# A ring of eight weight tiles in the first expert layer, and the second expert layer's weights loaded during the attention

## The reference, cut to what matters

```
# layer 0, experts: 8 experts, 128 -> 512 -> 128
h = relu(einsum('tc,efc->tef', x, w1) + b1)
y = einsum('tef,ecf->tec', h, w2) + b2          # two of 8 taken by the router, weighted
# layer 1, attention: 128 -> 128
A, x_el, sidegate, gate = four projections of the RMS-normalized rows
h = gated_scan(A, x_el * sidegate); y = (gate * h) @ w_o + residual
# layer 1, experts: 16 experts, 128 -> 256 -> 128
mag, freq = fx @ bank_mag, fx @ bank_freq
hidden = tanh(mag) * cos(softplus(freq) + 0.1 + bank_phase)
out = hidden @ bank_down                         # two of 16, weighted, then RMS norm
```

## Time and profile before

| | |
|---|---|
| median of 3 runs | 742.98 us (738.69 to 751.54) |
| the profiled execution | 746.29 us |
| its span, first to last instruction | 744.5 us |
| mean granted TensorE clock | 0.855 |
| experts of layer 0, first to last tile | 312 to 447 us of the span |
| attention of layer 1 | 450 to 510 us |
| router and sorting for layer 1 | 510 to 556 us |
| experts of layer 1 | 556 to 722 us |

### The profile page before, as it was taken

The page is one execution under the profiler, slowest core; times in us unless marked ns, Lnnn a source line. Parts: engine busy times, 40 slices in busy tenths (PEclk is TensorE's granted clock), DMA queues, the critical chain, the costliest instruction groups (busy, mean ns, idle before and its releaser), DMA issues.

```text
span 744.5 us, 9210 instructions
## 1 busy us (share of the span) xinstructions
PE 547.2 (73%) x2152; PEld 331.9 (45%) x2153; DVE 489.2 (66%) x911; ACT 332.0 (45%) x643; POOL 437.8 (59%) x329
## 2 busy tenths in 40 slices
PE   8678899989988897747666794697476777478730
PEld 4223234334333334446656791255144565356620
DVE  4898988998997996613522245368832777755527
ACT  4637646745753641112122245745014867960004
POOL 0275999988989982165455545217046773067760
PEclk9979989989989997669899797989758999686785
DMA  5431534333333400246455644001001123311115
GB/s 175 131 99 61 169 115 165 101 107 115 102 113 99 127 15 25 71 115 174 156 162 167 193 150 120 0 1 29 28 25 47 37 41 21 113 43 42 43 48 164
DMA packets 45437, 69.05 MB, mean 93 GB/s; under 512 B 6162, under 2 KB 25460, under 8 KB 45268
## 3 DMA queue, kind: packets, MB, share of 16 engines
q1 hardware_dynamic: 39828, 57.17, 24.9%
q0 software_dynamic: 5568, 11.41, 6.1%
HBM read 59.45 MB, written 9.11 MB: 92 GB/s over the span
## 4 chain that ended last, share of the span: by engine, by line
PE 41%; DVE 22%; issue 11%; ACT 9%; another core or an unknown queue 9%; DMA 2%; POOL 2%; DVEq 2%; ACTq 1%; SPq 0%; POOLq 0%
PE ps L1084 9%; DVE hs L1691 7%; PE ps L1210 4%; PE ps L1392 3%; PE ps L1221 3%; PE ps L1047 3%; PE ps L1078 3%; PE ps L1261 2%; PE ps L1356 2%; DVE prod L1701 2%; PE ps L1381 2%; ACT ps L677 2%; PE ps L1000 1%; PE ps L1361 1%
## 5 line engine op out<-in xcount | busy, mean ns | idle before, releaser
L490 POOL TENSOR_TENSOR bu<-uT,b_sb 128x1024 f32<-128x1024 f32 x62 | 146.0, 2375 | 29.6 <-DMA b_sb<-b_rows 29.6
L462 POOL DMA_INDIRECT y_dram<-ys,rows_i x87 | 90.7, 1042 | 97.0 <-DVE ys L1787 43.8
L456 POOL DMA_INDIRECT xl<-h_dram,rows_i x87 | 91.6, 1053 | 69.1 <-DVE rows_i L1573 37.5
L1084 PE MATMUL ps<-prod,cst 128*128 128x512 f32 x256 | 129.9, 652 | 2.9 <-DVE yT L1711 2.9
L677 ACT ACTIVATE ps<-dtT,neg_a 128x512 f32<-128x512 f32 x128 | 85.6, 685 | 61.2 <-DVE hs L1691 60.4
L501 POOL TENSOR_TENSOR prod<-hs,c_sb 128x1024 f32<-128x1024 f32 x32 | 76.8, 2399 | 28.7 <-PE ps L1084 19.0
L1084 PEld LDWEIGHTS ps<-prod,cst 128*128 128x128 f32 x256 | 50.3, 207 | 81.7 <-issue 76.7
L1691 DVE TENSOR_TENSOR_SCAN hs<-ps,carry,bu 128x512 f32<-128x512 f32 x64 | 77.6, 1264 | 4.7 <-ACT ps L677 4.6
L1221 PE MATMUL ps<-w_s,ht 128*128 x312 | 49.5, 309 | 38.4 <-ACT ht L779 19.8
L1691 DVE TENSOR_TENSOR_SCAN hs<-ps,bu 128x512 f32<-128x512 f32 x64 | 73.9, 1206 | 4.8 <-ACT ps L677 4.7
L779 ACT ACTIVATE ht<-ps,b1T 128x128 f32<-128x128 f32 x78 | 24.3, 363 | 97.0 <-remote 49.2
(11 more groups left out here) (264 smaller groups left out, 956.7 us busy)
## 6 DMA issues: line engine op xcount, KB each, us to landing
b_sb<-b_rows SPq DMA_DIRECT2D x31, 512.0 KB, 4.5
w1r<-in_w SPq DMA_DIRECT2D x39, 256.0 KB
c_sb<-b_rows SPq DMA_DIRECT2D x32, 256.0 KB, 3.6
mf_s<-in_mf SPq DMA_DIRECT2D x16, 256.0 KB
w_s<-in_w SPq DMA_DIRECT2D x9, 256.0 KB, 4.0
h_dram<-h_tok SPq DMA_DIRECT2D x8, 256.0 KB
phase_s<-in_phase SPq DMA_DIRECT2D x16, 128.0 KB
down_s<-in_down SPq DMA_DIRECT2D x1, 2048.0 KB, 7.2
```

What stands on the lines that cost most here:

```text
L456: pool.indirect_dma_start(xl[:, j % slots, :], None, h_dram[l], bass.IndirectOffsetOnAxis(ap=rows_i[:, 0, j:j + 1], axis=0)).then_inc(load ...
L462: pool.indirect_dma_start(y_dram[l], bass.IndirectOffsetOnAxis(ap=rows_i[:, 1, j:j + 1], axis=0), ys[:, j % XR, :], None).then_inc(saved[j ...
L490: nc.gpsimd.tensor_tensor(bu[:, g % RING, :, :], uT[:, c % 2, :, :], b_sb[:, k % BRING, g % 2, :].unsqueeze(1).broadcast_to([P, ND, CHUNK] ...
L1084: last = nc.tensor.matmul(bank(Y_BANK + d), ident, prod[:, g % RING, d, :], start=n == 0, stop=n == NS - 1)
```

## The change

`WR` goes from 3 to 8: SP loads the weights of up to eight tiles ahead. The ring then takes all of the region up to `w2_s`; `wmod_s` and what follows it are placed on top of it, and `signs`, used during the stage, has a second copy `signs2` at the place of the (then unused) sorting tables. The semaphores of the b and c rows of the scan are used again for the ring. The 32 loads behind tiles 3 to 34 go; in their place SP issues 16 loads (8 of `mf_s` with 512 KB, 8 of `phase_s` with 256 KB) right behind the eight loads of `y0a` and `y0b`. ACT's two scalings move from the end of the expert stage to behind the last `columns_router`, ahead of the wait for `pick_exp`.

```diff
-WR = 3
+WR = 8
...
         w1r, e = place("w1r", [P, WR, F0], at=f0_at)
-        wmod_s, e = place("wmod_s", [P, 2, 6 * C], at=e)
+        assert e <= f0_at + E0 * F0 * 4
+        wmod_s, e = place("wmod_s", [P, 2, 6 * C], at=f0_at)
...
+        signs2, _ = place("signs2", [P, 2, BATCH, C], at=y0_at)
...
-        b_loaded = [sem(f"b_loaded{u}") for u in range(BRING)]
-        c_loaded = [sem(f"c_loaded{u}") for u in range(CRING)]
+        streamed = [sem(f"streamed{u}") for u in range(max(WR, BRING + CRING))]
...
-                sp.dma_start(w1r[:, j % WR, :], w1[:, bass.ds(e, 1), :].rearrange("p a f -> p (a f)")).then_inc(w1_loaded[j % WR], 16)
-                if WR <= j < WR + 2 * E1:
-                    es = slice((j - WR) // 2, (j - WR) // 2 + 1)
-                    if (j - WR) % 2 == 0:
-                        sp.dma_start(mf_s[:, es, :], mf[:, es, :]).then_inc(S["in_f1"], 16)
-                    else:
-                        sp.dma_start(phase_s[:, es, :], phase[es, :].partition_broadcast(P)).then_inc(S["in_phase"], 16)
+                sp.dma_start(w1r[:, j % WR, :], w1[:, bass.ds(e, 1), :].rearrange("p a f -> p (a f)")).then_inc(streamed[j % WR], 16)
...
             for c in range(NCHUNK):
                 load_rows(0, ST0, c, y0)
+            for e in range(0, E1, 2):
+                es = slice(e, e + 2)
+                sp.dma_start(mf_s[:, es, :], mf[:, es, :]).then_inc(S["in_f1"], 16)
+                sp.dma_start(phase_s[:, es, :], phase[es, :].partition_broadcast(P)).then_inc(S["in_phase"], 16)
...
-            act.wait_ge(S["in_f1"], 16 * E1)
-            act.wait_ge(S["in_phase"], 16 * E1)
-            nc.scalar.activation(mf_s[:, :, H1:2 * H1], mf_s[:, :, H1:2 * H1], ACT.Copy, scale=1.0 / (2 * PI)).then_inc(S["phase_done"], 1)
-            nc.scalar.activation(phase_s[:, :, :], phase_s[:, :, :], ACT.Identity, bias=eps_s[:, 2:3], scale=1.0 / (2 * PI)).then_inc(S["phase_done"], 1)
             act.preload_act_table_set(LOG_EXP)
...
             columns_router(3)
+            act.wait_ge(S["in_f1"], 16 * (E1 // 2))
+            act.wait_ge(S["in_phase"], 16 * (E1 // 2))
+            nc.scalar.activation(mf_s[:, :, H1:2 * H1], mf_s[:, :, H1:2 * H1], ACT.Copy, scale=1.0 / (2 * PI)).then_inc(S["phase_done"], 1)
+            nc.scalar.activation(phase_s[:, :, :], phase_s[:, :, :], ACT.Identity, bias=eps_s[:, 2:3], scale=1.0 / (2 * PI)).then_inc(S["phase_done"], 1)
             act.wait_ge(S["pick_exp"], 2)
```

More of the change, by code:

```diff
@@ L317, in adaln_two_layers, with rows_streamed, w1_streamed @@
         gathered = [sem(f"gathered{c}") for c in range(NCHUNK)]
-        b_loaded = [sem(f"b_loaded{u}") for u in range(BRING)]
-        c_loaded = [sem(f"c_loaded{u}") for u in range(CRING)]
+        streamed = [sem(f"streamed{u}") for u in range(max(WR, BRING + CRING))]
         saved = [sem(f"rows_out{u}") for u in range(XR)]
-        w1_loaded = [sem(f"w1_loaded{u}") for u in range(WR)]
+        def rows_streamed(u):
+            if u < BRING:
+                return len(range(u or BRING, PAIRS, BRING))
+            return len(range(u - BRING, PAIRS, CRING)) if u < BRING + CRING else 0
+        def w1_streamed(j):
+            return 16 * (rows_streamed(j % WR) + j // WR + 1)
         def rounds(l, u):
@@ L387, in _ @@
                     if k:
-                        sp.dma_start(b_sb[:, k % BRING, :, :], b_rows[c, n:n + 2, :].partition_broadcast(P)).then_inc(b_loaded[k % BRING], 16)
+                        sp.dma_start(b_sb[:, k % BRING, :, :], b_rows[c, n:n + 2, :].partition_broadcast(P)).then_inc(streamed[k % BRING], 16)
                     if k >= CRING:
                         sp.wait_ge(S["prod_pool"], k - CRING + 1)
-                    sp.dma_start(c_sb[:, k % CRING, :], b_rows[c, NS + n + 1, :].partition_broadcast(P)).then_inc(c_loaded[k % CRING], 16)
+                    sp.dma_start(c_sb[:, k % CRING, :], b_rows[c, NS + n + 1, :].partition_broadcast(P)).then_inc(streamed[BRING + k % CRING], 16)
                     for dst, src, done in later[k - 4:k - 3] if k >= 4 else ():
@@ L486, in inputs @@
                 k = g // 2
-                pool.wait_ge(b_loaded[k % BRING], 16 * (k // BRING + (1 if k % BRING else 0)))
+                pool.wait_ge(streamed[k % BRING], 16 * (k // BRING + (1 if k % BRING else 0)))
                 if g >= RING:
@@ L496, in products @@
                 k = g // 2
-                pool.wait_ge(c_loaded[k % CRING], 16 * (k // CRING + 1))
+                pool.wait_ge(streamed[BRING + k % CRING], 16 * (k // CRING + 1))
                 pool.wait_ge(S["scan_done"], 2 * g + 2)
@@ L1203, in up0 @@
                 pe.wait_ge(S["xt_sb0"], j + 1)
-                pe.wait_ge(w1_loaded[j % WR], 16 * (j // WR + 1))
+                pe.wait_ge(streamed[j % WR], w1_streamed(j))
                 if j >= 2:
@@ L1624, in one_more, with bounded @@
                 then(nc.vector.tensor_scalar(mod[:, l, :, k, :], mod[:, l, :, k, :], 1.0, None, ALU.add))
-            def bounded(l, k):
-                g, s0, s1 = mod[:, l, :, k, :], signs[:, 0, :, :], signs[:, 1, :, :]
+            def bounded(l, k, s):
+                g, s0, s1 = mod[:, l, :, k, :], s[:, 0, :, :], s[:, 1, :, :]
                 nc.vector.tensor_scalar(s0, g, 0.0, 2.0, ALU.is_ge, ALU.mult)
@@ L1737, in _ @@
                     one_more(0, CB)
-                    bounded(0, GA)
+                    bounded(0, GA, signs)
                 if g == 4:
@@ L1793, in attention_weights @@
                 one_more(1, CB)
-                bounded(1, GA)
-                bounded(0, GB)
-                bounded(1, GB)
+                bounded(1, GA, signs2)
+                bounded(0, GB, signs2)
+                bounded(1, GB, signs2)
                 dve.wait_ge(S["in_l1"], 32)
```

## The result

| | before | after |
|---|---|---|
| median of 20 runs each | 743.48 us (736.14 to 751.54) | 744.09 us (740.22 to 751.32) |
| mean of the same 20 | 743.26 us | 744.98 us |
| the profiled execution | 746.29 us | 751.32 us |

The comparison's ratio, changed kernel to kernel before, is 1.0067, with a 95% interval of 1.0037 to 1.0097. That is slower by 0.67%: within 2% of no change, but of the other sign than forecast (0.9940). The ratio leaves out executions of each kernel that lie over 1.5% above its own quickest, four of the kernel before and at most one of the changed kernel, and this makes the difference larger; the means of all 20 differ by 0.23%, the medians by 0.08%. So the first question is whether the 0.67% is real.

The account below looks back on a forecast made before the run. Layer 0's expert stage was taken as bound by POOL's runs of indirect DMAs alternating with late PE signals. 746.3 less 1.5 (ring) and 3 (fewer loads) gave 741.8 us profiled, 738.5 as a median; range 719 to 750.

Parts of the forecast that it names:

- 1.5 us for the ring: Layer 0's experts: eight weight slots take away PE's waits for weights, between 0.5 and 8.5 us; 1.5 taken.
- 3 us for the loads that leave the stage: Layer 0's experts: less SP traffic may make holds begin later or end sooner; between nothing and 22 us, 3 taken.
- What bounds the stage: Layer 0's experts: POOL's runs of indirect DMAs alternate with holds, 3.3 us a tile; late weights are not the cause.
- holds: In the experts: PE's signal reaches other engines only when POOL's run of indirect DMAs has drained; tile 18's came 5.65 us late.
- Rival A: Layer 0's experts: stalls are streamed weights or their traffic and go; POOL the floor, 22 us saved, median 720; chance 0.24.
- Only when POOL's run has drained: Experts: PE's late signal gets through after POOL's run ends; ACT let go 1.3 us later at tile 18, 1.9 at the opening.
- rival B: Stage's opening: five more loads ahead of the gathers delay first tiles by up to 5.7 us; 745 to 756; chance 0.13.
- Rival C: Layer 0's experts: holds go by POOL's runs alone, the change does nothing; median 741.5; chance 0.63 together with the forecast.
- The moved loads at 0: Attention: the moved 6 MB land at 495, before ACT needs them at 519; cost 0, upper end 2 us.
- the scalings at 0: Ahead of L870: ACT's 14.64 us of idle time cover the moved scalings' 7.3 us; no gain at the old place, cost 0.
- five tiles and 16.4 us: Layer 0's experts: spacing between holds, three times 16.4 us for 5 tiles each, read as 3.3 us a tile.

Follow-up runs that it names:

- rows_by_sp: Changed kernel with layer 0's 39 gathers taken from POOL, SP loading consecutive rows instead of the chosen ones: 702.91 us, 0.9445 to the kernel before.
- layout_only: Changed kernel's placement and semaphores, but SP only three tiles ahead, 32 loads and scalings where they were before: 698.01 us, 0.9999 to the kernel before.
- again: The changed kernel once more, nothing altered, in job 1: 697.37 us, 0.9981 to the kernel before.
- no_stream: Changed kernel without the weight loads of tiles 8 to 38, which are multiplied with old weights: 741.27 us, 0.9982 to the kernel before.
- move_only: Kernel before, ring still three, with only layer 1's loads and scalings moved: 694.49 us in job 1, 0.9969 to the kernel before.
- move_only_h: Same kernel as move_only, measured again in job 3 on a chip with holds: 739.53 us, 0.9998 to the kernel before.

## Why the prediction was wrong, point by point

The forecast was a gain of 4.5 us, from two terms: 1.5 us for the ring and 3 us for the loads that leave the stage. The ratio of 0.9940 that they make lies outside all five intervals measured for the changed kernel. Both terms failed.

**What bounds the stage: right in the main.** The stalls of ACT are not weights: with every wait for weights at 51 ns, 40.8 us of "remote" remain, and with the loads for tiles 8 to 38 left out the stage takes 132.0 us. They are signals of PE that come late while POOL runs indirect DMAs: in one execution (`rows_by_sp`) the holds go from the stage that loses its gathers and stay in the one that keeps them. Rival A, chance 0.24, is out as an effect of this change.

**"Only when POOL's run has drained": too strong.** In the first two profiles every late signal came 0.9 to 3.1 us behind the end of a run. But in seven of the thirteen profiles with holds at least one came while the run went on, 15 of 175 late signals in all, by over 0.3 us and up to 4.7 us before its end. The prediction's own already has one: ACT is let go at 565.07, and POOL's run ends at 565.27. Why a signal gets through in the middle of a run, no run here shows.

**Rival A's price: too small.** The prediction gave 22 us for a stage with POOL as its floor. On the chips without holds the stage is 99 us, 36 less than in the first profile. The sum stopped at the 26 tiles that gather and the idle time in front of them. The 12 write-backs behind them, from the 27th at 421.35 us to the last at 447.23, took 25.9 us where POOL alone needs 15.4.

**"Ring of eight. I take 1.5": the waits were sized right, and taking them away bought nothing.** In the first profile four waits lie above 51 ns, by 1.4 us in all, and all of them went. But PE's waits are not on the path that sets the stage's length: `layout_only` has 12.7 us of them and the same 99.0 us as `again`. In return the ring has a cost that the sum had at nothing and only rival B had: five loads stand ahead of the first gathers. B's mechanism is there in all nine profiles with eight slots filled at once (third tile at 10.8 to 11.3 us) and in none of the other nine with the opening of three (9.7 to 9.8). Its price was mis-sized: not 5.7 us of issue time, but 1.1 to 1.5 at the third tile. On chips with holds the ninth write-back stands 44.1 to 45.4 us behind the first gather in six profiles with the opening of three (mean 44.5) and 45.4 to 46.2 in five with eight (mean 45.8), 1.3 us later. At the stage's end it is lost in the spread: 127.3 to 135.0 us and 129.5 to 132.7.

**"32 loads fewer in the stage. I take half of that, 3": not borne out.** The reason given, that a hold began sooner with SP's traffic (3.1 us into the run) than without (13.2), rested on two holds of different stages. `no_stream` takes the traffic away and has fifteen late signals where the changed kernel has twelve. The best estimate is 0. By time alone 3 us is not excluded: `move_only` gave 0.9969 (0.9927 to 1.0011) and 0.9998 (0.9956 to 1.0040), where 3 us would be 0.996. Rival C, that the change does nothing because the holds go by POOL's runs, comes nearest.

**The moved loads at 0, the scalings at 0: right.** The attention took 85.7 us after 86.6, and 86.0 in `move_only_h`; the scalings fill idle time of ACT at either place.

**The sum.** With 0 for both gains and 0 to 1.3 us for the opening it is 746.3 plus 0 to 1.3 us: no change, or up to 0.2% slower, and not 4.5 us faster. In three measurements with holds the changed kernel gave 1.0067, 1.0035 and 0.9988, in two without 0.9981 and 1.0015, and the kernel before against itself 0.9984 and 0.9970. The first, the only one whose interval does not hold 1, is the largest of five. What stays open is whether there is a true cost of 1 to 2 us on chips with holds; 12 executions a kernel, which spread over 10 us and more, do not decide that. That the cause would be the opening is likely by the profiles, and not shown in the time.

**The measure I took for given.** The prediction read one execution's holds, five tiles and 16.4 us, as the stage's pace. Two more profiles of the same kernel, in other jobs, have the late signals on other tiles, and stages of 128.6 and 129.9 us. A gain of 3 us was argued from a pattern that moves by 6 between executions.

## What to carry to other kernels

Ask of a stall labelled "remote" not only which signal is late but what the other engines did meanwhile: here the weights' own wait row (51 ns) excluded them at once, and POOL was in a run of indirect DMAs when the matmuls of 172 of the 175 late signals ended. Count the late signals themselves and not the label: ACT's waits at "remote" are 28.4 us in `no_stream` with fifteen late signals and 40.8 us in the changed kernel with twelve. Before a wait is put into a sum as a gain, ask whether its engine sets the stage's length: where another queue is slower (on the chips without holds 78 indirect DMAs at 1.28 us, one behind the other), a deeper ring gives nothing. The only edit here that moved the time by over 1% took DMAs off that queue, at the price of other rows. And look first at the part whose work no edit touches: when the scan alone varies by 12 us between executions, half a percent needs more than one comparison.

## What was not expected of the hardware

The same kernels run at two levels. The five jobs ran on five chips. On two of them signals of PE reached ACT about 0.14 us behind the modelled end of the matmuls in nearly every tile, and never over 0.43 us, through an unbroken run of 78 indirect DMAs; on the other three, 12 to 16 tiles of 39 were over 2 us late. This is worth 28 to 34 us in layer 0's stage (99 against 127 to 133), some 16 us in layer 1's experts (from the first gather to the end 180 against 194 to 198), and 46 us in all (696 against 742), many times what the change could do. Each chip had one job, so that it is the chip, and not the time at which the job ran, is likely and not shown. POOL's time for one such DMA is the same on both kinds, 0.97 us and 0.30 between. So nearly every hold goes with a run of POOL's, and such a run is not enough for one; what else it takes was not found, and no run here can show it.

Two sentences of the Trainium skill bear on the reading. "Perfetto Trace Analysis", in "Tensor Engine Instruction (MATMUL, LD_WEIGHTS)", puts the raising of the signal behind PSUM's acknowledgement, after the end that the profiler models; the 0.14 us agree, and no cause for a delay of 5 us is given there. The same page, in "DMA Instruction — SWDGE (GPSIMD)", says that the profiler's end of such a DMA is the end of descriptor generation and not of the transfer; the opening run and tile 18's run in the first two profiles, which end 1.2 to 2.3 us ahead of the release, agree with work that goes on behind a run's end; the signals that came inside a run are not explained by it.
